# First convolution: row and column sums of the images as TensorE products of the normed rows with a 0/1 matrix, VectorE left with the maxima

## The reference

```python
def _L0_conv_ref(x, conv_w, conv_b, gn_w, gn_b):
    g = x.reshape(b * GROUPS, cg, h, w)
    def conv1x1(t):
        return jnp.einsum('oi,bil->bol', conv_w, t) + conv_b[None, :, None]
    def branch(ph, pw):
        hw = conv1x1(jnp.concatenate([ph, pw], axis=2))
        ah, aw = (hw[:, :, :h], hw[:, :, h:])
        gated = g * sigmoid(ah)[..., None] * sigmoid(aw)[:, :, None, :]
        return gnorm(gated)
    x1 = branch(g.mean(axis=3), g.mean(axis=2))
    y1 = branch(g.max(axis=3), g.max(axis=2))
    x11, y11 = x1.reshape(b * GROUPS, cg, h * w), y1.reshape(b * GROUPS, cg, h * w)
    x12, y12 = softmax(x1.mean(axis=(2, 3))), softmax(y1.max(axis=(2, 3)))
    weights = einsum('bc,bcl->bl', x12, y11) + einsum('bc,bcl->bl', y12, x11)
    return (g * sigmoid(weights).reshape(b * GROUPS, 1, h, w)).reshape(b, c, h, w)
x = x + _L0_conv_ref(_ln_c(x), ...)
```

## Time and profile before

| | |
|---|---|
| median of 3 runs | 1151.49 us (1150.26 to 1151.76) |
| the profiled execution | 1151.33 us |
| its span, first to last instruction | 1149.6 us |
| TensorE matmul busy | 878.1 us (76%) |
| VectorE busy | 750.4 us (65%) |
| ScalarE busy | 575.9 us (50%) |
| GpSimd busy | 503.5 us (44%) |
| mean granted TensorE clock | 0.866 of full |

### The profile page before, as it was taken

The page is one execution under the profiler, slowest core; times in us unless marked ns, Lnnn a source line. Parts: engine busy times, 40 slices in busy tenths (PEclk is TensorE's granted clock), DMA queues, the critical chain, the costliest instruction groups (busy, mean ns, idle before and its releaser), DMA issues.

```text
span 1149.6 us, 25137 instructions
## 1 busy us (share of the span) xinstructions
PE 878.1 (76%) x7033; PEld 740.0 (64%) x7033; DVE 750.4 (65%) x1814; ACT 575.9 (50%) x1246; POOL 503.5 (44%) x412
## 2 busy tenths in 40 slices
PE   5321085874499999999964826599999999999975
PEld 4201064861288888888853712488888888888863
DVE  5899878999544444444446799466766767766540
ACT  4538266884245445444451466354564554655433
POOL 1198000000247667666661410354655655656640
PEclk8655599895599999999996965799999999999996
DMA  8248265784255565555659136656555464434438
GB/s 266 74 146 296 105 199 195 244 282 116 49 135 105 97 101 99 98 101 96 102 91 297 38 110 157 120 127 142 120 101 143 73 146 78 69 73 78 74 59 292
DMA packets 196629, 152.24 MB, mean 132 GB/s; under 512 B 97056, under 2 KB 181480, under 8 KB 196456
## 3 DMA queue, kind: packets, MB, share of 16 engines
q1 hardware_dynamic: 156536, 108.48, 33.1%
q0 software_dynamic: 27472, 38.97, 20.5%
q10 hardware_dynamic: 12576, 4.26, 1.4%
HBM read 92.35 MB, written 39.91 MB: 115 GB/s over the span
## 4 chain that ended last, share of the span: by engine, by line
PE 35%; DMA 25%; DVE 18%; issue 11%; SPq 4%; ACT 3%; DVEq 1%; POOL 1%; ACTq 1%; POOLq 0%
PE bank L857 14%; PE bank L830 12%; DMA columns<-region 8%; DMA region<-rows_x,region 8%; SPq L419 3%; DMA rows_y<-region 3%; PE bank L912 2%; DVE columns L1296 2%; DVE region L1275 2%; DMA tok<-rows_y 2%; DVE region L1273 2%; PE bank L734 2%; DMA wreg<-in_L_ffn_w_dram 1%; DVE wreg L261 1%; PE bank L812 1%
## 5 line engine op out<-in xcount | busy, mean ns | idle before, releaser
L830 PE MATMUL bank<-columns,wreg 128*128 x3360 | 382.8, 274 | 26.9 <-DMA columns<-region 26.8
L830 PEld LDWEIGHTS bank<-columns,wreg 128*128 128x128 f16 x3360 | 330.2, 98 | 68.9 <-issue 28.5
L583 POOL DMA_INDIRECT rows_y<-region x140 | 242.0, 1729 | 161.0 <-ACT region L1172 99.2
L530 POOL DMA_INDIRECT region<-rows_x,region x148 | 155.9, 1053 | 252.2 <-DVE region L1572 141.4
L857 PE MATMUL bank<-wreg,region 128*128 128x256 f16 x1680 | 189.2, 273 | 10.4 <-DVE region L1701 10.3
L857 PEld LDWEIGHTS bank<-wreg,region 128*128 128x128 f16 x1680 | 163.5, 98 | 32.1 <-DVE region L1701 13.4
L1157 ACT ACTIVATE region<-bank,b_t,wreg 128x256 f32<-128x256 f32 x280 | 137.3, 558 | 25.9 <-PE bank L830 25.5
L1706 DVE TENSOR_TENSOR region<-region 128x256 f16<-128x256 f32 x140 | 50.1, 420 | 107.2 <-ACT region L1164 107.2
L1172 ACT ACTIVATE region<-region 128x256 f32<-128x256 f32 x70 | 31.7, 500 | 163.4 <-DVE region L1713 163.4
L1701 DVE SCALAR_TENSOR_TENSOR region<-region,wreg 128x512 f16<-128x512 f32 x140 | 105.2, 751 | 5.0
L845 PE MATMUL bank<-wreg,region 128*128 (+1 forms) x864 | 100.2, 273 | 1.9 <-ACT region L1164 1.9
(11 more groups left out here) (285 smaller groups left out, 1156.0 us busy)
## 6 DMA issues: line engine op xcount, KB each, us to landing
wreg<-in_L_ffn_w_dram SPq DMA_DIRECT2D x112, 512.0 KB, 6.0
rows_x<-region SPq DMA_DIRECT2D x16, 512.0 KB, 6.5
rows_y<-tok SPq DMA_DIRECT2D x16, 512.0 KB, 6.8
tok<-rows_y SPq DMA_DIRECT2D x16, 512.0 KB, 6.8
wreg<-in_x_dram SPq DMA_DIRECT2D x4, 1024.0 KB, 9.4
out_dram<-columns ACTq DMA_DIRECT2D x16, 256.0 KB, 2.4
region<-rows_x,region POOLq DMA_INDIRECT x148, 2.9
columns<-region SPq DMA_TRANSPOSE x148
```

The costliest lines, as they stand in the source:

```text
L530: nc.gpsimd.indirect_dma_start(x_bits[:, b, r, 0:C + 2], None, rows_x[f], bass.IndirectOffsetOnAxis(ap=row_list, axis=0)).then_inc(xr_load ...
L583: nc.gpsimd.indirect_dma_start(rows_y[f], bass.IndirectOffsetOnAxis(ap=now[:, b, g_, 1:2], axis=0), (y_pair[:, b], y_rows)[f][:, g_, :], N ...
L830: last = pe.matmul(to, block, x_cols[:, bass.ds(b, 1), :, xs_, k, :].rearrange("p j r n -> p (j r) n"), start=(k == 0 and ws_ + xs_ == 0), ...
```

## The change

The normed tiles of the first block no longer go through the small buffer `xn` but into `norm_rows`, room for all 32 tiles, in the place of the loaded images. Before its first statistics VectorE writes a matrix of zeros and ones, `line_of`: for each of the two tiles of an image, 128 tokens by 32 columns, a one where the token lies in that row (columns 0 to 15) or in that column of the image (16 to 31). After the turns TensorE multiplies: 2 halves of the channels x 16 images x 2 tiles, weights a piece of `norm_rows`, moving operand `line_of`, sums in the banks `zb[2]` and `zb[3]`. ScalarE copies each bank to `line[:, 0, k]` after its first four squares. TensorE waits for these copies (`small_ready`) before it multiplies by `conv_bd`. VectorE keeps the four reductions of the maxima, and `lines_ready` counts only them. TensorE's loop over the turns is written out.

```diff
+        norm_rows = x_in.rearrange("p b k n -> p (b k n)").rearrange("p (t c) -> p t c", c=C)
+        line_of = region[:, 6144:6208].rearrange("p (h l) -> p h l", h=UT)
...
-                        last = pe.transpose(to[:, k, h * P:(h + 1) * P], xn[:, j, h, k * P:(k + 1) * P], ident[:])
+                        src = xn[:, j, h] if s == 1 else norm_rows[:, 4 * i + 2 * j + h]
+                        last = pe.transpose(to[:, k, h * P:(h + 1) * P], src[:, k * P:(k + 1) * P], ident[:])
...
-            pairs(pe, turn_normed)
-
+            for i in range(HB):
+                turn_normed(i)
+
+            pe.wait_ge(lines_known, 1)
+            for k in range(KC):
+                for u in range(NB):
+                    for h in range(UT):
+                        last = pe.matmul(zb[2 + k][:, u * 2 * HW:(u + 1) * 2 * HW], norm_rows[:, UT * u + h, k * P:(k + 1) * P],
+                                         line_of[:, h], start=(h == 0), stop=(h == UT - 1))
+                last.then_inc(lines_known, 1)
             pe.wait_ge(bd_ready, 1)
             for r in range(2):
                 for k in range(KC):
-                    pe.wait_ge(lines_ready, 2 * (r * KC + k) + 2)
+                    if r == 0:
+                        pe.wait_ge(small_ready, 2 + k)
+                    else:
+                        pe.wait_ge(lines_ready, 2 * k + 2)
...
             squares(0, 4)
+            for k in range(KC):
+                act.wait_ge(lines_known, 2 + k)
+                act.activation(line[:, 0, k].rearrange("p b l -> p (b l)"), zb[2 + k][:], ACT.Copy).then_inc(small_ready, 1)
             for r in range(2):
...
             def norm(s, i, j):
-                if s % 2:
-                    free(dve, rows_ready[j], HB * (s // 2) + i)
-                free(dve, xn_turned[j], HB * s + i)
+                if s == 1:
+                    free(dve, rows_ready[j], i)
+                    free(dve, xn_turned[j], HB + i)
                 for h in range(UT):
                     t = 4 * i + 2 * j + h
-                    last = dve.tensor_scalar(xn[:, j, h], tok[:, bass.ds(t, 1), :].rearrange("p a b -> p (a b)"),
+                    to = xn[:, j, h] if s == 1 else norm_rows[:, bass.ds(t, 1), :].rearrange("p a c -> p (a c)")
+                    last = dve.tensor_scalar(to, tok[:, bass.ds(t, 1), :].rearrange("p a b -> p (a b)"),
...
+            dve.wait_ge(consts, CONSTS)
+            chain(dve.memset(line_of, 0.0))
+            by_row, by_column = ident[:].rearrange("p (m w) -> p m w", w=HW), ident[:].rearrange("p (m w) -> p w m", w=HW)
+            for h in range(UT):
+                dve.tensor_reduce(line_of[:, h, 8 * h:8 * h + 8], by_row, AX.X, ALU.add)
+                last = dve.tensor_reduce(line_of[:, h, HW:2 * HW], by_column, AX.X, ALU.add)
+            last.then_inc(lines_known, 1)
...
-            for r, op in enumerate((ALU.add, ALU.max)):
-                for k in range(KC):
-                    v = g[:, k, :].rearrange("p (b h w) -> p b h w", b=NB, h=HW)
-                    dve.tensor_reduce(line[:, r, k, :, 0:HW], v, AX.X, op).then_inc(lines_ready, 1)
-                    if r + k:
-                        dve.tensor_reduce(line[:, r, k, :, HW:2 * HW], v.rearrange("p b h w -> p b w h"), AX.X, op).then_inc(lines_ready, 1)
-                        continue
-                    half, n = g[:, k, :].rearrange("p (b n) -> p b n", b=NB), L // 2
-                    while n > HW:
-                        chain(dve.tensor_tensor(fold[:, :, 0:n], half[:, :, 0:n], half[:, :, n:2 * n], op))
-                        half, n = fold, n // 2
-                    dve.tensor_tensor(line[:, r, k, :, HW:2 * HW], half[:, :, 0:HW], half[:, :, HW:2 * HW], op).then_inc(lines_ready, 1)
+            for k in range(KC):
+                v = g[:, k, :].rearrange("p (b h w) -> p b h w", b=NB, h=HW)
+                dve.tensor_reduce(line[:, 1, k, :, 0:HW], v, AX.X, ALU.max).then_inc(lines_ready, 1)
+                dve.tensor_reduce(line[:, 1, k, :, HW:2 * HW], v.rearrange("p b h w -> p b w h"), AX.X, ALU.max).then_inc(lines_ready, 1)
```

More of the change, by code:

```diff
@@ L233, in bass_metaformer @@
         xn_ready, xn_turned, xt_ready, xt_used = sem2("xn_ready"), sem2("xn_turned"), sem2("xt_ready"), sem2("xt_used")
+        lines_known = sem("lines_known")
         bd_ready, lines_ready, gates_psum, sig_ready = sem("bd_ready"), sem("lines_ready"), sem("gates_psum"), sem("sig_ready")
```

## The result

The changed kernel takes 1156.99 us (median of 20 runs, 1150.49 to 1165.44) against 1151.74 of the kernel before (20 runs, 1147.58 to 1157.27): a ratio of 1.0052, 95% interval 1.0034 to 1.0070, so slower by half a per cent. Its profiled execution has a span of 1154.4 us. The stage ends, with the first L1235, at 136.74, 5.2 us later than before (131.52).

A forecast was written before the change was run, and what follows sets the result against it. It took the stage to be bound by VectorE's chain of work, intertwined with GpSimd's products. GpSimd's first product at 65.7 plus 73.15 gives 138.85 against 131.52, +7.3 us, so a median of 1158.8 us, range 1150.5 to 1162.

The forecast's parts named there:

- 0/1 matrix hidden: VectorE's memset and four small reductions at the start fit its idle time until 8.73: priced nothing, 2 us at most uncovered.
- clock falls behind it by: TensorE's clock, full after dense turns, falls to half 3.7 us into the narrow sums, from a span of 2.5 to 3.7.
- 128 records: TensorE's 64 float32 sum matmuls, two records each: 33 at full clock, 95 at half, together 24.0 us, ending at 62.5.
- from there to S: From the sums' end to GpSimd's first product: result wait, ScalarE's copy, sigmoid table, sigmoid and handover, 3.2 us.
- S: Start of GpSimd's first product in the stage: forecast at 65.7, 12.5 us later than the 53.22 before.
- held: VectorE's two small tensor_scalars at S + 21.5 wait for GpSimd's third product, until S + 23.3, as a product would.
- E: Start of the first instruction behind the stage: forecast at S + 73.15 = 138.85, against 131.52 before.
- (e), the wait for the second half: ScalarE's copy of half 1's sums, then table load and sigmoid, delay GpSimd's first product: 62.5 + 3.2 = 65.7.
- (f), the order: Turns of GpSimd's and VectorE's products after S: stage ends at S + 73.15 if the tensor_scalars are held, S + 66.7 if free.
- Rival 1: Clock falls but VectorE's tensor_scalar pair is not held: stage ends at 132.4, +0.9 us, 1152.4; chance 0.20.
- Rival 2: TensorE's clock stays up through the sums: S = 56.0, end 129.15 with the hold, -2.4 us, 1149.1; chance 0.09.
- Rival 3: Narrow float32 matmuls cost 0.32 a record at half clock: sums of 37 us, S = 79, +20 us, 1172; chance 0.06.

The follow-up runs named there:

- e1: Changed kernel with the signs put on the max gates by ScalarE instead of VectorE's tensor_scalar pair: 1154.15 us, ratio 1.0016.
- e8: Changed kernel with a 128-column unit matrix as moving operand in place of the 32 columns, real sums left out: 1151.36 us, ratio 0.9987.
- f1: Changed kernel with the 0/1 matrix padded with zeros to 128 columns, all sums kept: 1152.44 us, ratio 1.0007.
- e2: Changed kernel with each image's four sum matmuls right behind its turns, not behind all turns: 1168.43 us, ratio 1.0141.
- e3: Changed kernel with a one-column sigmoid before ScalarE's copies of the sums, to load the table early: 1159.62 us, ratio 1.0062.
- e6: Changed kernel with half 0's gate product behind half 1's first image, each sigmoid right behind its half's copy: 1146.48 us, ratio 0.9959.
- c1: The kernel before, unchanged, measured again as a control: 1154.95 us, ratio 1.0014.
- e9: The kernel before with the signs put on the max gates by ScalarE: 1155.05 us, ratio 1.0038.

## Why the prediction was right

It said 1158.8 (1150.5 to 1162.0), slower with 0.68. Measured: 1156.99, slower. Step by step, in the profiled execution:

| step | predicted | after |
|---|---|---|
| 0/1 matrix hidden | nothing | statistics start at 8.67 (8.73 before) |
| first sum | 38.5 | 38.52 |
| clock falls behind it by | 3.7 us | 4.9 (in six executions with 32 columns twice 2.6 or 2.7, four times 4.5 to 4.9) |
| 128 records | 24.0 us | 22.94 (25.00 in e1) |
| from there to S | 3.2 | 2.8 |
| S | 65.7 | 64.26 (66.10 in e1) |
| VectorE's last maximum ends | 62.3 | 62.1 |
| L1306, now L1325 | held | held, 10.87 for 0.60 |
| E | S + 73.15 = 138.85 | S + 72.48 = 136.74 |

- **The clock.** Rows with 8 columns were taken as the nearest for 32, and 0.112 and 0.213 a record held. That the narrow matmuls do it, and not TensorE's load as such, was only argued; e8 and f1 show it, and e2 shows the other side. The moment of the fall is the term that was mis-sized: 3.7 lies between the 2.6 and 4.9 that I then saw, and it makes 2 us of S between one execution and the next. That the sums came within 1.1 us of 24.0 is in part luck: the 3.7 was taken from a fall behind idle time, not behind narrow matmuls.
- **(e), the wait for the second half.** The sum was nearly right (3.2, measured 2.8), the reason incomplete. I had the table load on the path and the gate product beside it, done 0.1 earlier. e3 shows the two as equal. The 0.3 us until the last result is there was an estimate that no row of the kernel before gave; the copy starts 0.03 us behind the end of the last matmul in the trace (61.46, 61.49), and that is most of what lies between 3.2 and 2.8. What made S late is that half 0's product and sigmoid stand behind half 1's sums and copy (e6: 12.8 us), and I took that order as given.
- **(f), the order.** I had both parts of L1306 wait for product 3 only, with the signs ready at S + 23.9. The second part waited for product 4 too (9.00 us), so the signs were ready at S + 32.3. VectorE's product then came at S + 32.4 behind product 4, as it had to in my order too: a wrong step that cost nothing. My sum had it at S + 32.8 by a slip. Product 4 was to be asked for 0.08 us behind product 3's end, S + 23.3, and so to end at S + 32.2; I added its 8.9 us to the moment of the signs, S + 23.9. That is the 0.6 to 0.7 us between S + 73.15 and the measured S + 72.48. Rival 1's sum for a pair that isn't held was right: S + 66.7, and 66.2 in e1, where the pair is gone. Its premise was wrong.
- **Rival 2** is what f1 makes come true, with the hold: S = 56.0 and E = 129.15 worked out, 55.45 and 127.89 measured. The gain of 2.4 us that it carried to the whole time does not show in f1's median.
- **Rival 3** found nothing: 32 columns cost no more than 8, nor do 128.
- **The whole time.** S came 1.4 us and E - S 0.7 us under the forecast, together 2.1 of the 7.3 forecast. The rest of the program passed the shift on: 5.2 us in the stage, 5.25 in the medians. So close an agreement is luck, since c1 has the same kernel 2.6 us apart.

On L1325 the Trainium skill (SBUF — State Buffer, "SBUF: two separate sides") has the rule that the ports which VectorE and GpSimd share are locked by one instruction for its whole length; the page's "Who interferes with whom" counts tensor_scalar among those that can take them, in a two-port mode. The traces agree with the lock: 1.95 and 9.00 us for 0.34, and 6.3 us less of stage without the pair. No run here shows the mode itself. e9 agrees with what the same section says, that the order of issue decides who blocks: 8.67 us instead of 4.43 for the product that came 2.8 us later.

## What to carry to other kernels

Moving 20 us of work off the engine that bounds a stage gained nothing here by itself; ask what the next engine's first instruction waits for, and look in the helper's own queue for work that stands in front of it without need. Where two engines exclude each other, the order of their requests is worth as much as the work: two small instructions that wait in the wrong place cost 6 us of the stage, and giving one engine its input earlier cost 5.4. Where narrow matmuls with a weight load each lose the clock, try wider ones: here 128 float32 columns took no longer a record than 32, and the clock that stayed up gave the stage 8.8 us. It shows in the granted clock by windows and not in the busy share. And expect a gain in one stage of a long program to be hard to see in its whole time, if it is no more than 3 us.

## What the runs showed of the hardware

- A float32 matmul that loads 128x128 weights takes 0.112 to 0.113 us a record at clock 1.00 with 128 moving columns (e8; f1, where up to three quarters of them are zeros) as with 32 (the changed kernel up to 43.4). With 32 the clock fell to 0.50 though the engine never paused, with 128 it stayed at 1.00 through the sums.
- float32 transposes alone raised the clock (1.00 in 30 to 32 of the changed kernel, with nothing else on TensorE since 25.7); four of them to eight 32-column records did not in 39 us (e2). The Trainium skill (TensorE: Matmul & The Clock Gate, "Part 4: PE-mode transpose") says that full clock doesn't engage for transposes in transpose mode; the trace here says otherwise for the float32 transposes of this kernel.
- Between two back-to-back instructions of VectorE that both wait for GpSimd's products, GpSimd's next product got in: in the changed kernel the second half of L1325 starts at 87.60 and takes 9.00 us, GpSimd's fourth product starts at 87.61 and takes its undisturbed 8.84.
